# Counting of parallel edges moved from a stage of its own into two attention sweeps of a four-layer graph network

## The reference, cut to what matters

```python
# layer 0: attention over the edges, 8 heads
score = einsum('ehd,ehd->eh', K[src], Q[dst]) / sqrt(16)
s = exp(clip(score, -5, 5))[:, :, None]
h_attn = segment_sum(V[src] * s, dst) / (segment_sum(s, dst) + 1e-6)
# output product, residual, batch norm, feed forward, batch norm
# layer 1: attention over the edges, 4 heads, softmax over each node's edges, skip gate, layer norm
# layer 2: four graph convolutions, each segment_sum(h[src] * norm, dst), layer norm between layers
# layer 3: two convolutions, each x + segment_sum(x[src], dst), then a two-layer product
```

## Time and profile before

| | us |
|---|---|
| median of 3 runs | 6949.93 |
| lowest and highest of them | 6941.06, 6957.64 |
| profiled execution, its own time | 6940.01 |
| span of the profiled execution | 6938.1 |
| TensorE busy | 5024.9 |
| VectorE busy | 3887.9 |
| GpSimd busy | 3682.3 |
| ScalarE busy | 2286.6 |

### The profile page before, as it was taken

One profiled execution on the slowest core, in us unless ns is written; L12 is line 12 of the kernel. 1 busy time (PEld: TensorE's weight loads), 2 busy tenths in 40 slices (PEclk: granted clock), 3 DMA queues, 4 the chain that ended last, 5 costly groups with the idle time before them and its releaser, 6 DMA issues. The chain is left out here.

```text
span 6938.1 us, 114758 instructions
## 1 busy us (share of the span) xinstructions
PE 5024.9 (72%) x23608; PEld 3891.1 (56%) x23609; DVE 3887.9 (56%) x9938; ACT 2286.6 (33%) x5605; POOL 3682.3 (53%) x4482
## 2 busy tenths in 40 slices
PE   5666666556666654666257777768999999999997
PEld 3455555224444443555221111118999999999997
DVE  4666666353333337887667777764444456444343
ACT  1111111111111110000128888873444444334432
POOL 3777777007777770000029999984444444334432
PEclk8988989775555556666565555559999999999999
DMA  4333333115555551333102222224343344323332
GB/s 126 98 98 97 98 98 98 29 43 156 158 158 156 158 151 33 96 95 91 38 19 74 74 75 74 75 85 151 141 151 141 141 160 168 111 105 139 135 130 76
DMA packets 523425, 745.71 MB, mean 107 GB/s; under 512 B 57861, under 2 KB 419336, under 8 KB 523240
## 3 DMA queue, kind: packets, MB, share of 16 engines
q1 hardware_dynamic: 440008, 512.24, 21.9%
q0 software_dynamic: 83232, 231.06, 11.9%
HBM read 584.89 MB, written 158.20 MB: 107 GB/s over the span
## 5 line engine op out<-in xcount | busy, mean ns | idle before, releaser
L1956 PE MATMUL ps<-moving,parts 128*128 128x384 f32 (+1 forms) x11662 | 2023.2, 332 | 78.5 <-POOL moving L1894 41.9
L1956 PEld LDWEIGHTS ps<-moving,parts 128*128 128x128 f32 x11662 | 1959.6, 189 | 111.3 <-issue 42.2
L444 POOL DMA_INDIRECT arena<-table_kv,arena x1664 | 1649.8, 991 | 520.3 <-issue 443.7
L1894 POOL CAST moving<-counts 128x1152 fp32r<-128x1152 uint8 (+1 forms) x833 | 944.5, 1134 | 1297.5 <-PE ps L1956 1246.7
L2019 ACT ACTIVATE moving<-counts 128x1152 fp32r<-128x1152 uint8 (+1 forms) x714 | 727.3, 1023 | 907.1 <-PE ps L1956 897.7
L1621 PE MATMUL ps<-arena 128*128 128x392 bf16 x1568 | 761.2, 505 | 366.0 <-ACT arena L1643 174.9
L1571 POOL TENSOR_SCALAR arena<-arena 128x128 bf16<-128x128 f16 x1568 | 1014.0, 660 | 0.1
L2162 DVE CAST moving<-counts 128x1152 fp32r<-128x1152 uint8 (+1 forms) x476 | 620.1, 1303 | 629.9 <-PE ps L1956 629.9
L1643 ACT ACTIVATE arena<-ps 128x392 uint8<-128x392 f32 x1568 | 812.4, 519 | 331.3 <-PE ps L1621 330.0
L1621 PEld LDWEIGHTS ps<-arena 128*128 128x128 bf16 x1568 | 163.5, 104 | 964.0 <-ACT arena L1643 752.4
L1586 DVE TENSOR_SCALAR arena<-arena 128x392 bf16<-128x392 f16 x1572 | 549.8, 350 | 199.9 <-PE ps L1621 197.8
(11 more groups left out here) (290 smaller groups left out, 5373.8 us busy)
## 6 DMA issues: line engine op xcount, KB each, us to landing
counts<-adjacency SPq DMA_DIRECT2D x105, 2352.0 KB, 8.5
adjacency<-arena SPq DMA_DIRECT2D x784, 98.0 KB, 1.7
edge_values<-arena SPq DMA_DIRECT2D x208, 256.0 KB, 3.2
arena<-edge_values SPq DMA_DIRECT2D x208, 256.0 KB, 3.1
arena<-table_kv,arena POOLq DMA_INDIRECT x1664
counts<-adjacency SPq DMA_DIRECT2D x14, 1568.0 KB, 6.5
table_kv<-arena POOLq DMA_DIRECT2D x14, 896.0 KB, 4.8
rest<-table_norm SPq DMA_DIRECT2D x60, 192.0 KB, 5.6
```

The lines of the kernel that those rows point to most:

```text
L444: pool.indirect_dma_start(m.ring4[:, r * HALF + k, 0:f], None, table, bass.IndirectOffsetOnAxis(m.idx4[:, r * HALF + k:r * HALF + k + 1], ...
L1894: pool.tensor_copy(to, of).then_inc(by_pool, 1)
L1956: mm = pe.matmul(m.bank(g % 2, n * P), d.parts[SOURCE[u]][:, s + q, t_, :], moving[:, q * n * P:(q + 1) * n * P], start=(s + q == 0 and t_ ...
```

## The change

The counting leaves its own stage. Its tiles become a class `Counting` of their own, `plan_windows` runs second, right after `plan`, and groups of counting are placed in the sweeps: two steps in each half of `attend` (104 groups in all), four steps in each half of `score` (208 groups). The last 80 of 392 groups run in `count_rest`, after `score`.

GpSimd has no part in the counting any more: VectorE makes both comparisons, for four steps at once, as two operations with two tensor inputs of 16 bits each (results 128x512 and 128x1568). The slot ring has 16 slots. Slots are no longer cleared: the first addition into a slot takes an extra slot as its other input, so each addition reads its own two register values (`to` and `of`). Registers are loaded per group, four from each of two partitions. Each addition waits for the one before it.

In the sweeps GpSimd's loop is written out, it reads row numbers straight from `m.src`, and the gather ring has eight slots (`RINGS`) in place of four. To make room, `m.x` is gone: `project1` loads x from DRAM by group and stores its result to a table `x0`, and `skip_gate` loads that and stores `x1`.

```diff
-RING = 32
+RINGS = 8
+RING = 16
+AT_GROUPS, SC_GROUPS = TURNS, 2 * TURNS
+WGROUPS = WSTEPS // HALF

+class Counting:
+        self.fours = split(sb("count_fours", HALF * WIDE, F16), WIDE, HALF)
+        self.by_lo = split(sb("by_lo", 2 * HALF * P, BF16), 2, P, HALF)
+        self.by_place = split(sb("by_place", 2 * HALF * WIDE, BF16), 2, WIDE, HALF)
...
+    def to(self, engine, regs, c):
+        engine.load(regs[:HALF], self.tables[0:1, ds(c * HALF, HALF)])
+        engine.load(regs[HALF:], self.tables[32:33, ds(c * HALF, HALF)])
+        at = [engine.snap(r, min_val=0, max_val=RING * WIDE // 2) for r in regs]
+        return at[:HALF], at[HALF:]

+def count_hot(dve, ct, c, r):
+    wait(dve, ct.product, (c - 1) * HALF)
+    dve.tensor_tensor(ct.by_lo[:, r % 2], ct.fours[:, 0:P, :], copies(ct.lo[:, ds(c * HALF, HALF)], 1, P), ALU.is_equal)
+    dve.tensor_tensor(ct.by_place[:, r % 2], ct.fours, copies(ct.place[:, ds(c * HALF, HALF)], 1, WIDE),
+                      ALU.is_equal).then_inc(ct.hot, 1)

+def count_add(dve, ct, c, r, k, to, of):
+    s = c * HALF + k
+    dve.wait_ge(ct.moved, s + 1)
+    wait(dve, ct.added, s)
+    dve.tensor_tensor(ct.slot_pairs[:, ds(to[k], WIDE // 2)], ct.slot_pairs[:, ds(of[k], WIDE // 2)],
+                      ct.counted_pairs[:, r % 2, k, :], ALU.add).then_inc(ct.added, 1)

+def count_product(pe, m, ct, c, r, k, bank, banks):
+    if k == 0:
+        pe.wait_ge(ct.hot, c + 1)
+    wait(pe, ct.moved, c * HALF + k - banks + 1)
+    pe.matmul(m.bank(bank, WIDE), ct.by_lo[:, r % 2, :, k], ct.by_place[:, r % 2, :, k], start=True, stop=True).then_inc(ct.product, 1)

+def count_move(act, m, ct, c, r, k, bank):
+    s = c * HALF + k
+    wait(act, ct.added, s - 2 * HALF + 1)
+    act.wait_ge(ct.product, s + 1)
+    act.activation(ct.counted[:, r % 2, k, :], m.bank(bank, WIDE), ACT.Copy).then_inc(ct.moved, 1)

+def gathers4(pool, m, table, free, gathered, before):
+    for j in range(2 * TURNS):
+        r = j % RINGS
+        wait(pool, free, j - RINGS + 1)
+        for k in range(HALF):
+            pool.indirect_dma_start(m.ring4[r][:, k * 2 * D:(k + 1) * 2 * D], None, table,
+                                    bass.IndirectOffsetOnAxis(m.src[:, j * HALF + k:j * HALF + k + 1], 0)).then_inc(gathered[r], 16)

 def attend, TensorE:
-                    pe.wait_ge(added, j * HALF + k + 1)
-                    mm = pe.matmul(m.bank(k, A0), ...)
+                pe.wait_ge(added, (j + 1) * HALF)          # once, ahead of the four products
+                    mm = pe.matmul(summed(k), ...)         # two results to a bank
                 turn(j + 2, (r + 2) % 4)
+                for k in (0, 1) if r % 2 == 0 else (2, 3):
+                    count_product(pe, m, ct, c, r // 2, k, 2 + k % 2, 2)
                 products(j, r)
                 queries(j + 2, r % 2)
 def attend, ScalarE: copy_indices goes, moves(...) of two steps comes in its place
 def attend, VectorE, at the head of a half and behind add(3):
-                    dve.wait_ge(used, j * HALF + k + 1)
+                    dve.wait_ge(used, (j + 1) * HALF)
+                if r % 2 == 0:
+                    count_hot(dve, ct, c + 1, r // 2 + 1)
+                else:
+                    count_stored(dve, ct, c, r // 2)
+                if not first:
+                    to_count, of_count = ct.to(dve, count_regs, c if r % 2 else c - 1)
...
                 add(3)
+                if not first:
+                    for k in (0, 1) if r % 2 else (2, 3):
+                        count_add(...)

 def score, VectorE:
             def half(i, j, r):
+                count_hot(dve, ct, j + (AT_GROUPS + 1), r + 1)
                 wait(dve, turned, j)
                 hits(...)
                 ... multiply, reduce as before ...
+                if not (isinstance(j, int) and j == 0):
+                    counts(j + (AT_GROUPS - 1), r + 3)     # ct.to, count_stored, four count_add
 def score, TensorE: four count_product between the transposes and the queries' products
 def score, ScalarE: copy_indices goes, four count_move come behind the copy
 def attend and score, SyncE: count_store, two stores to adjacency for a group

 def count_rest, VectorE, for 80 groups:
+                    count_hot(dve, ct, c + 1, r + 1)
+                to, of = ct.to(dve, regs, c)
+                count_stored(dve, ct, c, r)
+                for k in range(HALF):
+                    count_add(dve, ct, c, r, k, to, of)

 def project1: act.activation(m.x..., m.stage_b) goes; SyncE loads x and stores stage_b by group
 def skip_gate, VectorE and ScalarE:
-                wait(dve, xed, g)
+                wait(dve, turned, g)
+                wait(dve, xed, g * 16)                     # now the landing of a store
-                act.activation(m.x[:, ds(g * GN, GN)], m.stage_b[:, :], ACT.Copy).then_inc(xed, 1)
 def plan_windows:
-            pool.memset(m.slots, 0.0)                      # 34 slots of 392 bytes
+            pool.memset(ct.slots[:, :], 0.0)               # 18 slots
-    6 operations over 1,664 columns for the tables of the ring and of the clearing
+    3 for the table of `to`, 5 for the table of `of`, 3 copies that put the store's tables together

 def program:
         plan(nc, m, t)
+        plan_windows(nc, m, ct, t)
         project0(...)
         attend(..., ct, adj, ...)
         ...
         score(..., ct, adj, ...)
+        count_rest(nc, m, ct, adj)
         ...
         skip_gate(...)
-        plan_windows(nc, m, t, tables["x1"])
-        count_edges(nc, m, adj)
```

More of the change, by code:

```diff
@@ L170, in shared @@
         self.dst_rows = take(COLS)
-        self.ring4 = split(take(4 * HALF * 2 * D), 4 * HALF, 2 * D)
-        self.idx4 = take(4 * HALF, I32)
+        ring = take(4 * HALF * 2 * D)
+        n = HALF * 2 * D
+        after = rows[:, 0:n], rows[:, n:2 * n], pair[:, 0:n], self.stage_c[:, 0:n]
+        self.ring4 = ([ring[:, k * n:(k + 1) * n] for k in range(4)] + list(after))[:RINGS]
         self.hit4 = split(take(4 * HALF * P), 4, HALF, P)
@@ L607, in _, with half @@
             dve.sem_inc(added, HALF)
-            def half(i, j, h, r, first=False):
+            count_regs = registers(nc, dve, "at0ct", 2 * HALF)
+            def half(i, j, h, r, c, first=False):
                 if not first:
@@ L1258, in project1, with _ @@
         root = m.small[:, 330:330 + GB]
+        x = m.ring4[0][:, 0:GN]
+        @block.sync
+        def _(sp):
+            for g in range(GROUPS):
+                wait(sp, added, g)
+                sp.dma_start(blocks(x), group_rows(t["x"], g)).then_inc(x_in, 16)
+                sp.wait_ge(lned, g * GB + GB)
+                sp.dma_start(group_rows(x_table, g), blocks(m.stage_b[:, :])).then_inc(kept, 16)
+            sp.wait_ge(kept, 16 * (GROUPS + 1))
         @block.scalar
@@ L1603, in _, with group @@
-            for k in range(HALF):
-                one_hot(k, 0, k)
-            at = load_steps(dve, regs, m.ring, 0, (RING - 1) * WIDE // 2)
-            for r in range(4):
-                half(r, r % 2, at[r * HALF:])
-            with dve.Fori(1, WTURNS // 2) as i:
-                at = load_steps(dve, regs, m.ring, i * 4 * HALF, (RING - 1) * WIDE // 2)
+            regs = registers(nc, dve, "cedve", 2 * HALF)
+            def group(c, r, last=False):
+                if not last:
+                    count_hot(dve, ct, c + 1, r + 1)
+                to, of = ct.to(dve, regs, c)
+                count_stored(dve, ct, c, r)
+                for k in range(HALF):
+                    count_add(dve, ct, c, r, k, to, of)
@@ L1610, in _ @@
+            for c in range(first, first + 4):
+                group(c, c)
+            with dve.Fori(first // 4 + 1, WGROUPS // 4 - 1) as i:
                 for r in range(4):
-                    half(4 * i + r, r % 2, at[r * HALF:])
+                    group(4 * i + r, r)
+            for c in range(WGROUPS - 4, WGROUPS):
+                group(c, c, c == WGROUPS - 1)
         @block.tensor
         def _(pe):
-            def half(j, r):
-                for k in range(HALF):
-                    s = j * HALF + k
-                    pe.wait_ge(lo_hot, s + 1)
-                    pe.wait_ge(hot, s + 1)
-                    wait(pe, moved, s - UNROLL + 1)
-                    pe.matmul(bank(r % 2, k), m.by_lo[:, r, k, :], m.by_place[:, r % 2, k, :], start=True, stop=True).then_inc(product, 1)
@@ L1677, in _ @@
-            for r in range(4):
-                half(r, r, True)
-            with sp.Fori(1, WTURNS // 2) as i:
-                for r in range(4):
-                    half(4 * i + r, r)
-            for r in range(4):
-                sp.wait_ge(stored[r], 32 * (WTURNS // 2))
+            regs = registers(nc, sp, "cesp", 2 * HALF)
+            with sp.Fori(first // 4, WGROUPS // 4) as i:
+                for r in range(4):
+                    count_store(sp, ct, regs, adj, 4 * i + r, r)
+            for r in range(4):
```

(15 more changed lines are left out.)

404 lines of the change are left out of this document (195 added, 209 removed).

## The result

| | before | after |
|---|---|---|
| median, us | 6946.85 (4 runs, 6941.06 to 6957.64) | 6377.07 (4 runs, 6371.53 to 6382.56) |
| ratio, 95% interval | | 0.9185 [0.9173, 0.9196] |
| span of the profiled execution, us | 6938.1 | 6380.8 |
| mean granted clock of that execution | 0.757 | 0.817 |

The change makes the kernel 8.15% faster. The prediction said 6435 us, 58 us more than measured; its range of 6170 to 6700 and the likeliest case's own range of 6300 to 6600 hold the time.

What follows compares the result with a forecast made beforehand. The prediction took GpSimd issuing gathers to pace both sweeps, with room on VectorE. From 6940.0 us: -1065 counting stage, +229 score, +33 attend, +288 rest, +10 small items, giving 6435 us; range 6170 to 6700.

Steps and rivals of the forecast that it cites:

- the likeliest case: Whole kernel: the forecast of 6435 us, with its own range of 6300 to 6600 and a chance of 0.50.
- The stage that goes: Counting stage, paced by GpSimd: it ends in full when the counting moves, -1065 us.
- VectorE takes over the pace of score: Sweep of score: VectorE needs 6.1 us a half against GpSimd's 5.0 and more, +229 us.
- The price of comparisons: VectorE's two counting comparisons: 0.54 ns a column, 0.35 and 0.92 us, 1.27 us a group.
- The rival with full price: Counting comparisons on VectorE: repeated operands deny the 16-bit rate, +408 us, 6843 us in all; chance 0.13.
- the one that ends slower than before: Counting comparisons on VectorE: they cost still more than full price, 7270 us in all; chance 0.03.
- The chained additions: Counting's additions on VectorE: each waits for the one before, 0.50 us from addition to addition.
- Attend: Sweep of attend: a half goes from 5.37 to a mean of 5.53 us, +33 us.
- The rest: The 80 groups that run alone: 3.6 us each, +288 us.
- Small items: `plan_windows` +7 us, `skip_gate` +9 us, a shorter memset ending 5.3 us earlier, `project1` 0: together +10 us.
- the sweeps keep GpSimd's pace: Rival, both sweeps: registers hidden, additions 0.30 us, gathers set halves of 5.4 us; 6180 us; chance 0.18.
- The starved GpSimd: Rival, both sweeps: gathers not let in between gapless VectorE operations, halves 6.3 and 5.8 us; 6540 us; chance 0.13.

Runs made afterwards that it cites:

- e4: The changed kernel with three of four gathers left out in both sweeps, so its output is wrong: 6355.41 us in one run.
- e2: The changed kernel with score's two register loads moved from behind the reduction to behind the comparisons: 6258.49 us, ratio 0.9004.
- e9: e2 with attend's two register loads made once a group, in the odd half, behind the reduction and behind the comparisons for scatter: 6247.89 us, ratio 0.8976.
- e1: The changed kernel with all 392 groups of counting run alone and none in the sweeps: 7172.47 us in one run.
- e3: e2 with score's four additions spread around hits, multiplication and reduction instead of in a row: 6286.75 us, ratio 0.9047.
- e5: e2 with attend's registers loaded two at a time, behind the reduction and behind the comparisons for scatter: 6897.48 us, ratio 0.9115, in the slower second series.
- e6: e2 with four ring slots of gathered rows instead of eight: 6705.96 us, ratio 0.886, in the slower second series.

## Why the prediction was right, point by point

The total is 58 us off a change of 570. Score was put 37 us too dear, the rest 22 and the small items 6.5, the stage that goes 4 us too short; attend was put 17 us too cheap. So little of the closeness comes from errors that cancel, except in the small items, whose sum is near and whose parts are wrong.

**The stage that goes.** Right, -1069 for -1065: it was paced by one engine, and stages run one after another.

**VectorE takes over the pace of score.** Right, and shown: e4 takes most gathers away and the half hardly changes; e2 takes one cost of VectorE away and it changes by 0.6 us. The step on which it hung, that the registers stand behind the reduction's wait and are not hidden, is seen in the 0.87 us of idle time and undone by e2. The term was 0.20 us a half too large. Half of that is the way back from the last addition to the next comparison, 0.25 us on average where I wrote 0.35; the rest lies in the comparisons (1.22 for 1.27) and the additions (1.46 for 1.50).

**The price of comparisons.** 0.35 and 0.92 us were forecast; the next instruction starts 0.33 and 0.89 us later. The group line for the larger, after:

```profile
L252 DVE TENSOR_TENSOR by_place<-count_fours,count_place 128x1568 bf16<-128x1568 f16 x208 | 201.3, 968 | 0.0
```

Less the fixed 0.07 us, that is 0.82 us for 1568 columns, 0.52 ns a column, where I took 0.54, a little under the 0.57 of the additions. The rival with full price would have shown some 1.7 us here, and is refuted, with it the one that ends slower than before.

**The chained additions.** 0.49 us for 0.50. Their gap is 0.22 to 0.24 us in all the lines shown.

**Attend.** The direction was right and the term 17 us too small. The timeline, cut to the end of an even half and of the odd half behind it (the next multiplication L726 closes each), answers the earlier trace rows:

```profile
899.80 0.68 DVE L744 TENSOR_TENSOR arena<-arena 128x512 f32<-128x512 f32 x1
901.71 0.69 DVE L726 TENSOR_TENSOR arena<-arena,ps 128x512 f32<-128x512 f32 x1 [1.22 <-issue]
902.63 0.30 DVE L714 TENSOR_TENSOR arena<-arena,ps 128x137 f32 x1 [0.24 <-PE ps L625]
...
905.63 0.68 DVE L744 TENSOR_TENSOR arena<-arena 128x512 f32<-128x512 f32 x1
906.40 0.43 DVE L251 TENSOR_TENSOR by_lo<-count_fours,count_lo 128x512 bf16<-128x512 f16 x1
906.74 0.97 DVE L252 TENSOR_TENSOR by_place<-count_fours,count_place 128x1568 bf16<-128x1568 f16 x1
907.63 0.69 DVE L726 TENSOR_TENSOR arena<-arena,ps 128x512 f32<-128x512 f32 x1
```

From the weighting L744 to the next multiplication I had 1.6 us without comparisons and 2.0 with them; here it is 1.91 and 2.00, and over the sweep 1.8 and 2.2 on average. That is the mis-sized term: 0.2 us in each half. From multiplication to weighting I had 3.73 us, and on average it is 3.54 in an even half and 3.68 in an odd one, which gives part of it back. The wait of L714 for all four products, which I put at nothing, is the 0.24 us at 902.63; over the sweep it comes to 12.7 us in 29 waits. It was right to put it at nothing here, where the register loads delay the multiplication; e9 shows that it is the next limit, 92.8 us, once they don't.

**The rest.** 3.33 us a group for 3.6. In its timeline the additions start 1.57 us after the comparisons do (1.75 forecast), and again the way back is 0.26 or less for 0.35:

```profile
3101.64 0.42 DVE L251 TENSOR_TENSOR by_lo<-count_fours,count_lo 128x512 bf16<-128x512 f16 x1
3101.98 0.97 DVE L252 TENSOR_TENSOR by_place<-count_fours,count_place 128x1568 bf16<-128x1568 f16 x1
3103.21 0.26 DVE L272 TENSOR_TENSOR slots<-slots,counted 128x196 uint16 x1 [0.26 <-issue]
...
3104.66 0.26 DVE L272 TENSOR_TENSOR slots<-slots,counted 128x196 uint16 x1 [0.22 <-ACT counted L291]
3104.92 0.43 DVE L251 TENSOR_TENSOR by_lo<-count_fours,count_lo 128x512 bf16<-128x512 f16 x1
```

**Small items.** +3.5 for +10, and not for my reasons: `plan_windows` is 2.8 us shorter and `skip_gate`, which I charged with 9 us for the landing of its stores, 1 us shorter; `sum_values`, whose code is the same, is 6.8 us longer. It is not longer in e1. What makes it so in the changed kernel stays open.

**The rivals.** That the sweeps keep GpSimd's pace needed the registers hidden. In e3 VectorE's own sequence is well under the half, and the numbers given for this rival are nearly those measured: 5.48 us a half of score (5.4 forecast), gathers stretched by 0.46 us a half (0.40 forecast). In e2 the half is 5.31 and the stretch 0.29, but VectorE is as busy there as GpSimd. The starved GpSimd needed that a waiting gather isn't let in between two operations without a gap. The timeline of score refutes this at 2106.39, and so do all 42 gathers of that sweep that start in L252 and are held: each ends 0.82 us after L252 does, though `hits` follows without a gap.

## What to carry to other kernels

Work moved under another engine's pace is worth its own stage's length only as far as the receiving engine's sequence fits: write that engine's half down instruction by instruction, with sequencer work (register loads, chained waits) as terms of their own, since in this kernel one misplaced pair of register loads cost 118 us, where the whole change gained 570. Put such loads behind an operation that is long and waits for nothing, ahead of the wait that would expose them. Expect that a wait taken away uncovers the next: in attend the loads went, and the wait for TensorE's products took most of their place. And when VectorE works beside GpSimd's gathers, count the operations with two SBUF inputs, not VectorE's busy share: filling its idle gaps with them made e3 slower than e2.

## What the runs showed of the hardware

A gather that starts during a VectorE operation with two SBUF inputs ends 0.82 us after that operation's end, with 16-bit as with 32-bit operands, unless it starts so near the end that its own 0.95 us last longer. It is let in between two such operations that follow without a gap (the changed kernel at 2106.18). A multiplication with one input in PSUM and a reduction don't hold it: in the changed kernel's score 82 gathers start during L866 and 153 during L869, all of them with their plain 0.95 us. The rising mean of gathers (948 ns in e1, 1021 in e2, 1064 in e3, all in score) comes from such holds.

A comparison whose one operand repeats each row of four runs at 0.52 ns a column, about as fast as the additions with their plain 16-bit operands (0.57).

In the series in which the kernel before took 7565.52 us instead of 6950.07, GpSimd's mean wait between gathers of score in e5 was 0.65 us instead of e2's 0.30, and more than half of that time (308.5 of 534.5 us) is put down to SyncE's return of slots. Why those came late, and whether the ring of four or the other register loads kept e6 191.5 us under e5 there, was not settled; the third series didn't show the condition again.
